# Idle bf16 identity products at the seams of the second cross attention in a two-block Perceiver kernel

## The chip, the cores and the metric

The kernel runs on one core of a Trainium2 chip. The metric is the device time of one execution in microseconds (us), from launch to completion. The core has a matrix engine (TensorE, PE in the profile, whose weight loads are a row of their own, PEld), VectorE (DVE), ScalarE (ACT), GpSimd (POOL) and SyncE (SP), which here issues most DMAs. The engines run their own instruction streams and meet on semaphores. The profile gives the clock that was granted to TensorE as a share of full speed: 1.00 is 2.4 GHz, 0.50 is 1.2 GHz.

## The reference

The input is x (16 x 64 tokens, width 256) and a context (16 x 1024 tokens, width 256). Two blocks are applied, with a residual sum and a layer normalisation around each step:

```python
x = x + L0_xattn(ln(x), ctx, ctx, mask, ...)   # 16 heads of 16, masked keys
x = x + L0_attn(ln(x), ...)                    # linear attention, 16 heads of 64
x = x + L0_ffn(ln(x), ...)                     # binarised weights, scale, bias, clip
x = x + L1_xattn(ln(x), ctx, ctx, ...)         # causal: 64 queries see keys 0..63
x = x + L1_attn(ln(x), ...)                    # gated delta rule with convolutions
x = x + L1_ffn(ln(x), ...)                     # 8 experts, the best one per token

def L1_xattn(query, key, value, Wq, bq, ...):
    q = (query @ Wq.T + bq)...; k = (key @ Wk.T + bk)...; v = (value @ Wv.T + bv)...
    scores = einsum('bhtd,bhsd->bhts', q, k) / sqrt(D) + causal
    return (einsum('bhts,bhsd->bhtd', softmax(scores), v)...) @ Wo.T + bo
```

The second cross attention is causal over 64 queries, so only the first 64 of the 1024 context tokens matter to it.

## The kernel before

The 1024 tokens are eight tiles of 128 (NT = 8), the width is two chunks of 128 (KC = 2). The program is four stages, one after the other, each a block in which every engine has one hand-written stream: `stage_abc` (the whole first block, and the keys `d_k` and values `d_v` of the second cross attention), `stage_d` (the second cross attention, and the gates of the gated delta rule), `stage_e` (the gated delta rule) and `stage_f` (the experts). At the end of a stage every engine drains, the engines meet, GpSimd clears the semaphores of the stage, and they meet again (lines 76, 80 and 81 of the profile). Nothing of a stage starts before that.

At the end of `stage_abc` the last products on TensorE are the output projection of the linear attention (L1168) and one product for the feed-forward step of tile NT - 2 (L1176). The feed-forward steps of the last two tiles are finished on VectorE inside `stage_d`.

`stage_d` runs over tiles t = 0 to 7 with a software pipeline of several tiles. The names that are needed:

- TensorE, before the loop: `turn_x(0)` (L1462, two transposes of the normalised tile), `queries(0)` (L1469, four products for the queries, two records each), then the transposes of `xc` (L1542) for the feed-forward step of the last tile, which wait for VectorE.
- TensorE, in iteration t: `scores(t)` (L1478, four bf16 products that lay the causal mask into banks 0 to 3, then L1486, 32 small products), for t = 0 the product of the feed-forward step (L1551, `cproj`), `turn_x(t + 1)`, `project(t - 2)` (L1519), `turn(t - 1, 0)` (L1498), `queries(t + 1)`, `turn(t - 1, 1)`, `weigh(t - 1)` (L1509, 64 small products).
- ScalarE copies the transposes out (`d_xt`, L1282), writes the scaled and biased queries block by block (`d_qbd`, L1288, four instructions), takes the exponentials (L1297) and copies the turned probabilities out (`d_pt`, L1303). The first copy of `d_xt` stands behind waits for two small GpSimd operations (L1256).
- VectorE, in iteration t: `shift(t, r)` for r = 0, 1 (L1378, the row maxima; L1380, the subtraction), for t = 0 the rest of the feed-forward step of the last tile (L1421, L1397 to L1401, and the moments), then `lengths(t, r)` (L1385, L1388), whose inverses GpSimd multiplies in (L1270).

`stage_e` begins on TensorE with L2144 (products of 8 columns) and L2158, the projections: 32 records of 128x512 before the first wait for another engine. ScalarE takes the first 1024 columns after eight of those records (`tap`, L1773), and VectorE convolves (L1954).

Every instruction of the stages stands in the order in which it is written; there is no planner. PSUM is eight banks of 512 float32 columns: in `stage_d` banks 0 to 3 hold scores, bank 4 the turned probabilities, bank 5 (`m_bank`) the transposed input and the queries, banks 6 and 7 the weighed values and others. `c.identb` is the 128x128 identity in bf16, loaded at the start of `stage_abc`.

Of the kernel before, what the change touches and what calls it, by code (L numbers as in the profile page):

```python
# [16 lines left out]
P = 128  # L17
B, S, D = 16, 64, 256
# [128 lines left out]
def stage_abc(nc, c):  # L147
# [6 lines left out]
    with stage_semaphores(nc) as ctx:  # L154
# [91 lines left out]
        bank = [ctx.enter_context(nc.psum_tensor(f"a_bank{i}", [P, 512], F32)) for i in range(8)]  # L246
        q_banks, k_banks, v_banks, t_banks = bank[0:2], bank[2:4], (bank[5], bank[6]), (bank[4], bank[7])
# [562 lines left out]
        def _(pe):  # L810
# [293 lines left out]
            for t in range(NT + 1):  # L1104
                if 0 < t < NT:
                    pe.wait_ge(U["xt"], t + 1)
                    pe.wait_ge(U["qt"], t)
                    for i in range(2):
                        dense(t, bwq, q_banks, i, U["qproj"])
                if 0 < t <= NT:  # L1110
                    pe.wait_ge(U["kh"], t)
                    if t == 1:
                        pe.wait_ge(T["xout"], NT)
                        pe.wait_ge(T["ot"], B)
                    else:
                        pe.wait_ge(U["ot"], t - 1)
                    turn_heads(kh, t_banks, U["ktp"])
                if t == NT:
                    fill(0)
                    fill(1)  # L1120
                if 0 < t < NT:
                    if t > 1:
                        pe.wait_ge(U["xout"], t - 1)
                    if t > 2:
                        pe.wait_ge(C["scaled"], t - 2)
                        pe.wait_ge(C["xt"], t - 2)
                    pe.wait_ge(U["xt"], t + 1)
                    for i in range(2):
                        dense(t, bwk, k_banks, i, U["kproj"])
                if 0 < t <= NT:  # L1130
                    attend_scores(t - 1)
                if t == NT:
                    fill(2)
                    fill(3)
                if 0 < t < NT:
                    pe.wait_ge(U["v"], t)
                    for i in range(2):
                        dense(t, bwv, v_banks, i, U["vproj"])
                if 0 < t <= NT:
                    attend_values(t - 1)  # L1140
                if t == NT:
                    fill(4)
                    fill(5)
                if t < NT:
                    pe.wait_ge(U["qh"], t + 1)
                    turn_heads(qh, q_banks, U["qtp"])
                if 0 < t < NT - 1:
                    pe.wait_ge(U["kh"], t + 1)
                    pe.wait_ge(NB["xn"], t + 2)
                    turn_tile(k_banks[1][:, 0:256], t + 1, U["xtp"])  # L1150
                if t > 1:
                    pe.wait_ge(NC_["xn"], t - 1)
                    if t == NT - 1:
                        pe.wait_ge(U["kh"], t + 1)
                    if t > NT - 1:
                        pe.wait_ge(C["scaled"], t - 2)
                    turn_tile(k_banks[1][:, 256:512], t - 2, C["xtp"])
                if t == NT:
                    fill(6)
                    fill(7)  # L1160
                if 0 < t <= NT:
                    pe.wait_ge(U["ot"], t)
                    if t < NT:
                        pe.wait_ge(U["kh"], t + 1)
                    else:
                        pe.wait_ge(U["xout"], t - 1)
                    for a in range(8):
                        m = pe.matmul(k_banks[0][:, 0:D], otb[:, a, :], bwo[:, a, :], start=(a == 0), stop=(a == 7))  # L1168
                    m.then_inc(U["oproj"], 1)
                if t > 1:  # L1170
                    pe.wait_ge(C["binary"], 1)
                    pe.wait_ge(C["xt"], t - 1)
                    if t < NT - 1:
                        pe.wait_ge(U["xt"], t + 2)
                    for kk in range(KC):
                        m = pe.matmul(k_banks[1][:, 0:D], xtc[:, t % 2, kk, :], wt[:, kk, :], start=(kk == 0), stop=(kk == KC - 1))  # L1176
                    m.then_inc(C["proj"], 1)


def stage_kit(nc, ctx, tag, banks=True):  # L1180
# [14 lines left out]
def stage_d(nc, c):  # L1195
# [4 lines left out]
    with stage_semaphores(nc) as ctx:  # L1200
        sb, sem, sems, _ = stage_kit(nc, ctx, "d", banks=False)
        ps = c.ps
        bank = [ps[:, i * 512:(i + 1) * 512] for i in range(8)]
# [255 lines left out]
        def _(pe):  # L1459
            def turn_x(t):  # L1460
                for k in range(KC):
                    m = pe.transpose(m_bank[:, k * P:(k + 1) * P], c.xn[:, t, k * P:(k + 1) * P], c.ident[:, :])  # L1462
                m.then_inc(z["xtp"], 1)

            def queries(t):
                pe.wait_ge(z["xt"], t + 1)
                for k in range(KC):
                    for kk in range(KC):
                        m = pe.matmul(m_bank[:, 256 + k * P:256 + (k + 1) * P], c.d_wq[:, kk, k * P:(k + 1) * P],  # L1469
                                      xt[:, t % 2, kk, :], start=(kk == 0), stop=(kk == KC - 1))  # L1470
                m.then_inc(z["qproj"], 1)
# [60 lines left out]
            def constants():  # L1532
                for k in range(KC):
                    pe.matmul(bank[4][:, 0:D], c.col("e_b2", k).to_broadcast([P, P]), c.e_w2[:, k, :], start=(k == 0), stop=(k == KC - 1))
                for k in range(KC):
                    pe.matmul(bank[4][:, D:D + E], c.f_small[2][:, :], c.f_small[0][:, k, :], start=(k == 0), stop=(k == KC - 1))

            turn_x(0)
            queries(0)
            pe.wait_ge(z["cxn"], 1)  # L1540
            for k in range(KC):
                m = pe.transpose(bank[6][:, k * P:(k + 1) * P], xc[:, k * P:(k + 1) * P], c.ident[:, :])  # L1542
# [2 lines left out]
            for t in range(NT + 3):  # L1545
                if t < NT:
                    scores(t)
                if t == 0:
                    pe.wait_ge(z["cxt"], 1)
                    for k in range(KC):  # L1550
                        m = pe.matmul(bank[7][:, 0:D], xtc[:, k, :], c.c_wt[:, k, :], start=(k == 0), stop=(k == KC - 1))  # L1551
                    m.then_inc(z["cproj"], 1)
                if t + 1 < NT:
                    if t > 2:
                        pe.wait_ge(z["ht"], t - 3)
                    if t + 1 > NT - 3:
                        pe.wait_ge(z["cxn"], t - NT + 5)
                    turn_x(t + 1)
                if 1 < t < NT + 2:
                    project(t - 2)  # L1560
                if 0 < t <= NT:
                    turn(t - 1, 0)
                if t + 1 < NT:
                    queries(t + 1)
                if t > 3:
                    if t == 4:
                        pe.wait_ge(z["weights"], 224)
                    pe.wait_ge(z["ht"], t - 3)
                    pe.wait_ge(z["ot"], min(t - 1, NT))
                    if t > NT:  # L1570
                        pe.wait_ge(z["gate"], t - 4)
                    gates(t - 4)
                if 0 < t <= NT:
                    turn(t - 1, 1)
                if t > 3:
                    pe.wait_ge(z["xout"], min(t - 1, NT))
                    decay_inputs(t - 4)
                if t > 2:
                    u = t - 3
                    pe.wait_ge(z["h"], u + 1)  # L1580
                    pe.wait_ge(z["qbd"], min(t + 2, NT))
                    if u:
                        pe.wait_ge(z["ht"], u)
                    for k in range(KC):
                        m = pe.transpose(m_bank[:, k * P:(k + 1) * P], h[:, u % 2, k * P:(k + 1) * P], c.ident[:, :])
                    m.then_inc(z["htp"], 1)
                if 0 < t <= NT:
                    if t > 1:
                        pe.wait_ge(z["ot"], t - 1)
                        pe.wait_ge(z["xout"], t - 1)  # L1590
                    else:
                        pe.wait_ge(z["csc"], 1)
                    if t > 3:
                        pe.wait_ge(z["gate"], t - 3)
                    weigh(t - 1)
                if t == NT + 1:
                    constants()


LEVELS = 6  # L1600
# [1138 lines left out]
```

## Time and profile before

| | |
|---|---|
| median of three runs | 699.14 us (697.95 to 700.17) |
| the profiled execution | 700.65 us |
| its span, first to last instruction | 698.9 us |
| around the span | 1.75 us |
| mean granted clock of TensorE | 0.935 |
| TensorE busy | 610.0 us (87%) |
| VectorE busy | 382.4 us (55%) |
| ScalarE busy | 333.5 us (48%) |
| GpSimd busy | 128.1 us (18%) |

All stretches in this document are given in us from the start of the span. `stage_abc` ends at about 343, `stage_d` at about 431, `stage_e` at about 580. The profiled execution took 1.5 us more than the median of the runs.

### The profile page before, as it was taken

The numbers are of one execution on the slowest core, as the hardware profiler recorded it, in microseconds if no ns is written. First come the engines' busy times: TensorE is split into PE (matmuls) and PEld (weight loads), VectorE is DVE, ScalarE is ACT, GpSimd is POOL, SyncE is SP. The second block draws the span as 40 slices with busy tenths as digits, with TensorE's granted clock in tenths as the row PEclk, the third lists the DMA queues.
The fourth block names the chain that finished last, engine by engine and source line by source line (L and its number), as shares of the span: only waits on it lengthen the run. The fifth ranks groups of instructions, "written<-read, shape, count | busy, mean of one in ns | idle before, by whom it ended". The sixth has DMA issues, their size and how long they took to land. (4 is left out here: it accounts for less than half of the span.)

```text
span 698.9 us, 20484 instructions
## 1 busy us (share of the span) xinstructions
PE 610.0 (87%) x8420; PEld 455.6 (65%) x8420; DVE 382.4 (55%) x911; ACT 333.5 (48%) x927; POOL 128.1 (18%) x192
## 2 busy tenths in 40 slices
PE   4779998999899999999777988988798986599995
PEld 2447666665466666666656765465798876498995
DVE  6426788875434545552267884879565783011211
ACT  1325655553444455444246764655365263144451
POOL 2002221001200000000223443424520204011111
PEclk9869999999999999999868999999789996799999
DMA  5950000000700000000230000000000007996110
GB/s 152 306 203 2 3 2 2 2 17 27 165 2 1 2 1 2 1 1 2 61 104 1 3 3 1 0 3 3 2 3 1 1 1 278 323 378 197 26 33 19
DMA packets 32717, 40.78 MB, mean 58 GB/s; under 512 B 8031, under 2 KB 28000, under 8 KB 32385
## 3 DMA queue, kind: packets, MB, share of 16 engines
q1 hardware_dynamic: 28672, 32.24, 14.2%
q0 software_dynamic: 1520, 4.38, 1.9%
q10 hardware_dynamic: 2448, 3.09, 1.6%
q8 instruction: 54, 0.88, 0.5%
q14 instruction: 23, 0.18, 0.1%
HBM read 35.33 MB, written 4.90 MB: 58 GB/s over the span
## 5 line engine op out<-in xcount | busy, mean ns | idle before, releaser
L390 ACT ACTIVATE a_pr<-a_bank,a_nms 128x160 f32<-128x160 f32 x128 | 49.2, 392 | 41.2 <-DVE a_nms L726 38.1
L2485 ACT ACTIVATE f_hb<-f_bank,cols 128x128 f32<-128x128 f32 x96 | 31.1, 368 | 59.7 <-PE f_bank L2596 38.1
L2596 PE MATMUL f_bank<-f_xts,f_w 128*128 x384 | 46.9, 282 | 9.0 <-ACT f_hb L2485 8.2
L2596 PEld LDWEIGHTS f_bank<-f_xts,f_w 128*128 128x128 f32 x384 | 46.4, 198 | 10.0 <-ACT f_hb L2485 8.4
L2606 PE MATMUL f_bank<-f_w,f_hb 128*128 128x256 f32 x192 | 46.4, 385 | 0.8 <-DVE f_yb L2565 0.8
L630 DVE TENSOR_REDUCE a_negmx<-a_bank 128x2 f32<-128x320 f32 x64 | 30.4, 475 | 22.8 <-PE a_bank L863 22.8
L2606 PEld LDWEIGHTS f_bank<-f_w,f_hb 128*128 128x128 f32 x192 | 35.3, 194 | 5.1 <-DVE f_yb L2565 1.2
L2557 DVE TENSOR_SCALAR f_xts<-f_bank 128x256 f32 x12 | 5.1, 424 | 60.8 <-PE f_bank L2588 60.8
L360 POOL TENSOR_TENSOR a_spr<-a_linv,a_hm 128x128 f32<-128x128 f32 x32 | 12.1, 400 | 123.9 <-DVE a_linv L679 111.1
L974 PE MATMUL a_bank<-b_wq,a_xtb 128*128 128x512 f32 x64 | 30.6, 624 | 2.9 <-ACT a_ct L483 2.9
L627 DVE COPY a_pt<-a_bank 128x512 f32<-128x512 f32 (+1 forms) x48 | 28.5, 593 | 7.9 <-PE a_bank L872 5.3
L410 ACT ACTIVATE a_lnv<-ln_mv,a_eps 128x1 f32<-128x1 f32 (+1 forms) x23 | 6.8, 295 | 52.6 <-DVE ln_mv L552 52.5
L1954 DVE SCALAR_TENSOR_TENSOR e_cv<-de_ps,cols,e_cv 128x1008 f32<-128x1008 f32 (+2 forms) x24 | 29.6, 1246 | 4.1 <-ACT e_cv L1773 3.5
L872 PE MATMUL a_bank<-ident,a_pr 128*128 128x128 f32 x128 | 21.8, 296 | 10.1 <-DVE a_pt L627 6.9
L2158 PE MATMUL de_ps<-e_ht,e_wqkv 128*128 128x512 f32 x64 | 30.4, 628 | 0.0
L789 DVE TENSOR_TENSOR x<-x,a_bank 128x256 f32<-128x256 f32 x8 | 3.4, 421 | 48.9 <-PE a_bank L1168 48.9
L1252 POOL MEMSET d_eps<- 128x1 f32 x3 | 0.2, 99 | 163.3 <-POOLq L81 163.3
L974 PE MATMUL a_bank<-b_wv,a_xtb 128*128 128x512 f32 x64 | 29.9, 607 | 0.0
L1168 PE MATMUL a_bank<-b_wo,a_pr 128*128 128x256 f32 x128 | 29.6, 384 | 0.1
L755 DVE TENSOR_REDUCE a_ss<-a_qbd 128x16 f32<-128x1024 f32 x16 | 19.4, 1215 | 18.3 <-ACT a_qbd L471 18.3
L974 PE MATMUL a_bank<-b_wk,a_xtb 128*128 128x512 f32 x64 | 29.0, 593 | 0.0
L471 ACT ACTIVATE a_qbd<-a_bank 128x512 f32<-128x512 f32 x32 | 17.3, 594 | 21.7 <-PE a_bank L974 21.7
(406 smaller groups left out, 1457.8 us busy)
## 6 DMA issues: line engine op xcount, KB each, us to landing
f_w<-in_f_w SPq DMA_DIRECT2D x16, 1024.0 KB, 10.8
a_ct<-in_ctxt SPq DMA_DIRECT2D x15, 160.0 KB, 4.4
slots<-a_zero POOLq DMA_DIRECT2D x1, 2210.0 KB, 12.1
f_xs<-slots ACTq DMA_DIRECT2D x14, 130.0 KB, 2.4
rows<-in_rows SPq DMA_DIRECT2D x1, 1096.0 KB, 8.1
x<-in_x SPq DMA_DIRECT2D x2, 512.0 KB, 5.4
b_wq<-in_b_wq SPq DMA_DIRECT2D x1, 1024.0 KB, 6.2
b_wk<-in_b_wk SPq DMA_DIRECT2D x1, 1024.0 KB, 8.3
```

The costliest lines, as they stand in the source:

```text
L390: i = act.activation(pr[:, p, j, k, :], s_bank[j][:, k * KW:(k + 1) * KW], ACT.Exp, bias=nms[:, p, j, k:k + 1], accum_out=rsum[:, p, 2 * j ...
L627: dve.tensor_copy(pt[:, a:a + n, :].rearrange("p a n -> p (a n)"), src[:, 0:n * P]).then_inc(done, 1)
L630: dve.tensor_reduce(negmx[:, p, j, :], s_bank[j][:, 0:KC * KW].rearrange("p (k n) -> p k n", n=KW), AXX, ALU.max, negate=True).then_inc(ne ...
L755: dve.reduce_sum(ss[:, g, :], sq[g].rearrange("p (h n) -> p h n", n=DA), AXX).then_inc(done, 1)
L872: m = pe.transpose(dst[:, (2 * jj + k) * P:(2 * jj + k + 1) * P], pr[:, p, 2 * g + jj, k, 0:KM], c.ident[:, :])
L974: m = pe.matmul(banks[i][:, :], xtb[:, t % 2, kk, :], wx[:, kk, i * 512:(i + 1) * 512], start=(kk == 0), stop=(kk == KC - 1))
L1168: m = pe.matmul(k_banks[0][:, 0:D], otb[:, a, :], bwo[:, a, :], start=(a == 0), stop=(a == 7))
L1954: a = dve.scalar_tensor_tensor(o_[:, :, back:S], src[:, :, 0:S - back], c.col("e_cw", 4 * m + 3 - back), o_[:, :, back:S], ALU.mult, ALU.add)
L2158: a = pe.matmul(ps[:, at + 512 * g:at + 512 * g + 512], wqkv[:, kk, m * P:(m + 1) * P], ht[:, kk, 512 * g:512 * g + 512], start=(kk == 0), ...
L2485: act.activation(hb[:, m, :], bank[m % 4][:, 0:P], ACT.Gelu, bias=c.col("f_b1", e * FC + m)).then_inc(z["act"], 1)
L2596: j = pe.matmul(bank[m % 4][:, 0:P], w1[:, e, kk, m * P:(m + 1) * P], xts[:, bass.ds(i % 2, 1), kk, :].rearrange("p b n -> p (b n)"), star ...
L2606: j = pe.matmul(bank[5][:, 0:D], hb[:, m, :], w2[:, e, m, :], start=(m == 0), stop=(m == FC - 1))
```

## The change

A function `warm` is added. It issues n products of the bf16 identity with itself (128x128 by 128x128) into columns of a PSUM bank that nobody reads before they are written again. Nothing waits for these products and they wait for nothing but their place in TensorE's stream. They are issued at six places: 12 at the end of TensorE's stream in `stage_abc`, 4 ahead of `turn_x(0)`, 10 between `turn_x(0)` and `queries(0)`, 8 between `queries(0)` and the wait for `xc`, 4 between `scores(0)` and the wait ahead of `cproj`, and 12 at the end of TensorE's stream in `stage_d`. That is 50 products. Nothing else changes.

```diff
                         m = pe.matmul(k_banks[1][:, 0:D], xtc[:, t % 2, kk, :], wt[:, kk, :], start=(kk == 0), stop=(kk == KC - 1))
                     m.then_inc(C["proj"], 1)
+            warm(pe, c, t_banks[0][:, 0:P], 12)
+
+
+def warm(pe, c, dst, n):
+
+    for _ in range(n):
+        pe.matmul(dst, c.identb[:, :], c.identb[:, :], start=True, stop=True)
...
+            warm(pe, c, bank[7][:, D:D + P], 4)
             turn_x(0)
+            warm(pe, c, bank[7][:, D:D + P], 10)
             queries(0)
+            warm(pe, c, bank[7][:, D:D + P], 8)
             pe.wait_ge(z["cxn"], 1)
...
                 if t == 0:
+                    warm(pe, c, bank[4][:, 0:P], 4)
                     pe.wait_ge(z["cxt"], 1)
...
                 if t == NT + 1:
                     constants()
+            warm(pe, c, bank[0][:, 0:P], 12)
```

## Rows read from the trace of the kernel before

**Rows 1.** The page, section 2: busy tenths and clock in 40 slices of the span.

```profile
PE   4779998999899999999777988988798986599995
...
PEclk9869999999999999999868999999789996799999
```

**Rows 2.** Stretches around the seams: length, busy us (records) of each engine, clock, DMA share, GB/s.

```profile
342.05:344.58 2.53, 0.00 (x0) 0.03 (x1) 0.74 (x2) 0.00 (x0) 0.04 (x2) 1.00 0.00 0
344.58:358.28 13.70, 11.52 (x66) 8.58 (x66) 10.09 (x22) 5.39 (x16) 5.38 (x13) 0.50 0.70 209
358.28:365.11 6.83, 3.72 (x50) 3.01 (x50) 5.10 (x11) 4.71 (x13) 3.09 (x4) 1.00 0.00 0
365.11:371.94 6.83, 6.53 (x108) 5.27 (x109) 2.35 (x4) 1.80 (x5) 0.88 (x1) 0.50 0.01 2
...
432.25:436.79 4.54, 4.54 (x10) 2.26 (x11) 1.06 (x3) 1.89 (x5) 2.47 (x12) 0.62 0.00 0
```

**Rows 3.** Waits of VectorE in 344.58 to 360: total us, times, longest.

```profile
DVE d_ngm L1378 <- PE de_ps L1486: 2.8, 2, 1.7
```

**Rows 4.** Timeline of the seam between `stage_abc` and `stage_d`: start, length, engine, line.

```profile
341.02 1.03 PE L1176 MATMUL a_bank<-c_wt,a_xtc 128*128 128x256 f32 x4
...
342.43 0.40 DVE L556 TENSOR_SCALAR xnorm<-x,ln_mv,ln_rs 128x256 f32<-128x256 f32 x1
...
344.58 0.63 PE L1462 MATMUL de_ps<-ident,xnorm 128*128 128x128 f32 x2 [2.53 <-PEq L81]
...
345.08 0.52 POOL L1256 TENSOR_TENSOR d_bq<-d_sc,cols 128x2 f32<-128x2 f32 x2
...
345.63 0.38 ACT L1282 ACTIVATE d_xt<-de_ps 128x256 f32<-128x256 f32 x1 [7.21 <-POOL d_bq L1256]
```

**Rows 5.** Timeline of the first two tiles of `stage_d`.

```profile
346.07 2.08 PE L1469 MATMUL de_ps<-d_xt,d_wq 128*128 128x128 f32 x8 [0.86 <-ACT d_xt L1282]
...
348.19 1.51 ACT L1288 ACTIVATE d_qbd<-de_ps,d_bq,d_sc 128x128 f32<-128x128 f32 x4 [1.75 <-PE de_ps L1469]
...
348.77 0.69 PE L1542 MATMUL de_ps<-ident,d_xc 128*128 128x128 f32 x2 [0.62 <-DVE d_xc L1407]
...
350.24 1.99 PE L1486 MATMUL de_ps<-d_k,d_qbd 32*128 32x64 f32 x32
...
352.28 0.69 DVE L1378 TENSOR_REDUCE d_ngm<-de_ps 128x8 f32<-128x512 f32 x1 [1.73 <-PE de_ps L1486]
...
357.24 1.50 ACT L1288 ACTIVATE d_qbd<-de_ps,d_bq,d_sc 128x128 f32<-128x128 f32 x4 [1.13 <-PE de_ps L1469]
...
358.67 0.20 DVE L1388 RECIPROCAL d_linv<-d_lsum 128x8 f32<-128x8 f32 x1
...
359.98 0.69 DVE L1378 TENSOR_REDUCE d_ngm<-de_ps 128x8 f32<-128x512 f32 x1 [1.11 <-PE de_ps L1486]
...
365.41 1.17 PE L1509 MATMUL de_ps<-d_pt,d_v 64*32 64x64 f32 x64 [2.09 <-ACT d_pt L1303]
...
367.48 1.99 PE L1486 MATMUL de_ps<-d_k,d_qbd 32*128 32x64 f32 x32
```

**Rows 6.** TensorE's timeline of a later tile at the full clock.

```profile
375.54 0.93 PE L1509 MATMUL de_ps<-d_pt,d_v 64*32 64x64 f32 x64 [1.78 <-ACT d_pt L1303]
376.41 0.61 PE L1478 MATMUL de_ps<-d_causal,identb 128*128 128x256 bf16 x4
376.95 1.12 PE L1486 MATMUL de_ps<-d_k,d_qbd 32*128 32x64 f32 x32
...
379.58 1.06 PE L1469 MATMUL de_ps<-d_xt,d_wq 128*128 128x128 f32 x8
```

**Rows 7.** Timeline at 408.67: four bf16 weight loads at the full clock.

```profile
408.67 0.33 PEld L1478 LDWEIGHTS de_ps<-d_causal,identb 128*128 128x128 bf16 x4
```

**Rows 8.** Timeline of the seam between `stage_d` and `stage_e`.

```profile
430.37 0.41 PE L1585 MATMUL de_ps<-ident,d_h 128*128 128x128 f32 x2
430.83 0.38 ACT L1348 ACTIVATE e_ht<-de_ps 128x256 f32<-128x256 f32 x1 [1.94 <-PE de_ps L1585]
...
432.25 0.58 PE L2144 MATMUL de_ps<-e_wab,e_ht 128*128 128x8 f32 x4 [1.46 <-PEq L81]
...
438.10 1.11 ACT L1773 ACTIVATE e_cv<-de_ps,cols 128x1024 f32<-128x1024 f32 x1 [2.05 <-PE de_ps L2158]
439.25 1.27 DVE L1954 SCALAR_TENSOR_TENSOR e_cv<-de_ps,cols,e_cv 128x1008 f32<-128x1008 f32 x1 [3.54 <-ACT e_cv L1773]
```

## The prediction

> **What bounds the kernel now.** I read the page first. Its row of busy tenths has TensorE at eight or nine tenths in most slices, and the clock row under it dips in a few places [rows 1]; two of the dips lie where the change puts products. The reader is to see that TensorE is both the busiest engine and the only one whose speed changes. Next I cut the time around the two seams into stretches by clock [rows 2]. From 342.05 to 344.58 TensorE has no product at all, at clock 1.00. The next 13.70 us are granted 0.50, although TensorE is busy in 11.52 of them. A second fall comes at 365.11 after a thin stretch (3.72 us busy in 6.83) and lasts 6.83 us. A third piece of half clock lies in the first microseconds of `stage_e` (mean 0.62 over 4.54 us). Then I asked who waits for whom in the first cold stretch: VectorE, which carries the first two tiles, waits 2.8 us in two pieces for the scores [rows 3]. Elsewhere in it VectorE is busy for 10.09 of 13.70 us. So a slow TensorE costs time here, but not all that it loses.
>
> **The first seam.** The last real product ends at 342.05, VectorE's last operation at 342.83, and the engines start again at 344.5 [rows 4]. The hole is the handover between the stages, not a wait for data. Twelve products now follow the last real one. No row shows a bf16 product of 128 columns with a load of its own, so I bound its pitch. The four bf16 masks of 256 columns take 0.61 us at the full clock with the drain of the last [rows 6], so their pitch is about 0.11 us, which is also 256 columns at 2.4 GHz; that is the upper end. Half the columns at half of that, 0.055, is the lower end. Four bf16 loads take 0.33 us, or about 0.08 each [rows 7], and as every product has its load I take 0.08. Twelve are 0.96 us, so TensorE is done at 343.0 instead of 342.05. VectorE had released the meeting only at 342.83, which hides all but 0.15 us (nothing at 0.055, 0.5 us at 0.11). The hole shrinks from 2.53 to about 1.7 us.
>
> The Trainium skill, TensorE: Matmul & The Clock Gate, section Back-to-back issue gap, gives 81 ns for each product of 128 columns in a stream of loads and products. By that page twelve would take 0.97 us, and the sum would be the same.
>
> **The start of `stage_d`.** Four products ahead of `turn_x(0)` take 0.32 us. ScalarE's first copy starts at 345.63, released by GpSimd's L1256 and not by the transposes [rows 4], so at the full clock they are free: the transposes end at about 345.3. The ten after `turn_x(0)` are 0.8 us, from 345.1 to 345.9, and the queries could not start before 346.07 [rows 5]. The eight after `queries(0)` are 0.64 us, ahead of a wait for VectorE that lasts until 348.77; the queries end at 347.1 at the full clock, so these too are covered. The four after `scores(0)` delay `cproj`, which VectorE needs only after its two shifts.
>
> **What the clock gives back, if it stays.** Compare the same work at either clock: the queries take 2.08 us cold and 1.06 warm, 32 score products 1.99 and 1.12, four masks about twice their 0.61 [rows 5, 6]. The chain for tile 0 is: VectorE's `xc` at 348.77, its two transposes (pitch 0.11 in place of 0.21), four masks (0.43 in place of 0.85), scores. TensorE reaches the scores at about 349.5 instead of 350.24; their operands from ScalarE are there at 348.8, since the queries end one microsecond sooner. Scores then end 0.87 us faster. The first shift starts at about 350.65 in place of 352.28: 1.6 us gained. From there VectorE has 6.6 us of its own work (352.28 to 358.87 [rows 5]), and at 359.98 it begins the next shift after 1.11 us of waiting for the scores of tile 1. These waited for ScalarE's `d_qbd` at 357.24, itself released by TensorE's queries. Warm, the queries of tile 1 end near 353.6 and ScalarE is held by the exponential behind VectorE's second shift (the two shifts take four times 0.69, until 353.4), so `d_qbd` runs from 354.0 to 355.5 and the scores are ready at 356.7, before VectorE is (357.3). The 1.11 us go too. Together 1.6 + 1.1 = 2.7 us, almost the 2.8 of [rows 3]. What is late next is VectorE itself, up to 362. Later tiles follow VectorE by way of `d_pt` and `weigh(0)` at 365.41, so the head start is carried on.
>
> **The second seam.** TensorE's stream ends at 430.78, ScalarE's at 431.21 [rows 8]. Twelve products are 0.96 us and end at about 431.75, 0.5 us behind ScalarE (0.2 at 0.055, 0.9 at 0.11). This delays the handover: a real cost, with nothing over it. Against it, in this execution the clock was down for the early projections: eight records of 512 columns should take about 3.6 us, and the first tap started at 438.10, 5.4 us after the projections began. If the clock stays, some 1.6 us of that come back at the tap and at VectorE's convolution at 439.25, and after that VectorE sets the pace of its chain. I take 1.5.
>
> **The sum.** Against the profiled execution: 700.65 - 2.7 - 1.5 + 0.15 + 0.5 = 697.1, and 0.2 less for the smaller transposes and masks of tile 1 that I left out, so 696.9. The median of the runs shown is 1.5 us below the profiled execution. I read that as an execution that had one cold piece more than most, and the fall at the second seam, after a hole of only 1.5 us, is the likeliest of them. Then the median has 2.7 to give and pays 0.65: 699.14 - 2.7 + 0.65 = 697.1, or 696.9 with the same 0.2. Both ways meet.
>
> **The rivals.**
>
> (B) The products do not hold the clock. Half a hole is still there (1.7 us of 2.53). For it: at the second seam the clock fell after only 1.47 us without products. Against it: that hole stands beside thin products of 8 columns, while here the TensorE before it is dense, and fourteen products follow within a microsecond of the restart. Then only the costs stay: 699.14 + 0.65, and about 0.4 us at the ten products, which at half clock are 1.1 to 1.6 us in a gap of 0.86: 700.0 to 700.4. The section HAM oscillation of the same page of the Trainium skill warns of longer standstills than the one here; by it the clock would not have fallen at 344.58 even without the products and they would buy nothing. The row shows that it fell.
>
> (C) The clock holds, but less arrives. Runs in which the fall came at another moment lose less, and the second fall stays or moves so that it covers more. If only the 1.6 us of the first shift arrive: 699.14 - 1.6 + 0.65 = 698.2.
>
> (D) More arrives: the second fall at 365.11 goes as well. From `weigh(0)` to the end of the scores of tile 2 the cold clock took 4.06 us (365.41 to 369.47 [rows 5]), the same work warm 2.53 (375.54 to 378.07 [rows 6]). With the rest up to 371.94 that is 1.5 to 2.5 us: 694.4 to 695.4. Against it: the hole there, 2.09 us before `weigh(0)`, has no product in it.
>
> (E) Slower. The handovers are paid in full: pitch 0.11 or more, clock down all the same, so that each product costs 0.2 us. Then the second seam alone is 12 x 0.2 = 2.4 less 0.4 of cover, the first 2.4 less 0.8, the ten products 2.0 less 0.9 of gap: 2.0 + 1.6 + 1.1 = 4.7, or 703.8. It decides from a pitch of about 0.14 us, where the three come to 1.3 + 0.9 + 0.5 = 2.7 us with no gain.
>
> **How the numbers follow.** A measurement of this kernel tells about 0.3% (2.1 us) from no change: faster is below 697.0, slower above 701.2. The forecast (A), 696.9 with its own range from 696.2 to 697.6, has 0.38; as it sits on the edge I count 0.31 as faster and 0.07 as the same. B has 0.17 and C 0.21, both the same. D has 0.17, faster. E has 0.07, slower. Faster 0.48, same 0.45, slower 0.07. The range takes in C and most of D and reaches to the near end of B: 694.9 to 699.7.
>
> **What would show it.** In the profile of the changed kernel: a clock of 1.00 from the first seam to the second tile; twelve bf16 records behind L1176 at a pitch near 0.08 us; the restart of `stage_d` at most 0.2 us later against L1176; the queries at 1.06 us, not 2.08; VectorE's wait for L1486 down from 2.8 us to under 0.3; a clock of 1.00 at L2158 and the handover there 0.5 us longer. Wrong would be a clock that still falls before `queries(0)`, or a first shift of tile 1 that does not move by more than 2 us against the restart.

## The result and the profile after

| | before | changed |
|---|---|---|
| median of the runs beside each other (8 and 8) | 699.65 us | 696.05 us |
| the profiled execution | 700.65 us | 695.91 us |
| its span | 698.9 us | 694.1 us |
| mean granted clock | 0.935 | 0.946 |

The ratio is 0.9951, with a 95% interval from 0.9927 to 0.9974: 3.4 us faster, between 1.8 and 5.1. Repeated later on 12 runs it was 0.9970 (0.9940 to 0.9999), or 2.1 us. One of those 12, at 704.27 us, was a slow run and is left out of the ratio.

First the stretches of the changed kernel round the seams, with the same columns as [rows 2].

```profile
341.36:343.89 2.53, 0.67 (x13) 0.52 (x10) 0.75 (x3) 0.00 (x0) 0.04 (x2) 1.00 0.00 0
343.89:352.94 9.05, 7.16 (x89) 6.08 (x90) 7.68 (x14) 4.05 (x13) 5.26 (x12) 1.00 0.87 281
352.94:356.35 3.41, 2.04 (x40) 1.47 (x37) 3.20 (x9) 1.92 (x5) 0.41 (x1) 1.00 0.44 99
356.35:359.76 3.41, 2.77 (x14) 2.72 (x14) 3.31 (x8) 2.35 (x6) 1.64 (x2) 0.50 0.00 0
359.76:370.00 10.24, 6.21 (x131) 5.09 (x130) 6.62 (x15) 6.95 (x19) 2.32 (x3) 1.00 0.01 2
370.00:376.83 6.83, 6.83 (x110) 5.54 (x111) 3.58 (x8) 2.94 (x11) 4.56 (x5) 0.50 0.01 2
414.38:417.79 3.41, 3.41 (x10) 2.12 (x9) 2.00 (x5) 1.59 (x5) 2.06 (x2) 0.50 0.00 0
430.47:436.00 5.53, 5.53 (x16) 2.80 (x17) 1.28 (x4) 3.01 (x6) 3.23 (x14) 1.00 0.00 0
```

The cold 13.70 us behind the first seam are gone, and so is the half clock at the start of `stage_e`. But there is a new fall at 356.35, 12.5 us behind the restart, in the second tile; the old second fall comes later; and there is one at 414.38, 70.5 us behind the restart, that the profile before does not have. That last one need not be due to the products: the fourth start of the run without any of them, r1 below, has one 71.4 us behind its restart. Products at the seams do nothing about the holes behind them.

The timeline of the first seam and the first tile. L1184 is the line of the idle products, and the lines behind it are shifted by the new code: L1469 is now `turn_x` (L1462 before), L1476 answers to L1469 of before, L1552 to L1542, L1493 to L1486, L1385 to L1378.

```profile
340.33 1.03 PE L1176 MATMUL a_bank<-c_wt,a_xtc 128*128 128x256 f32 x4
...
341.19 0.83 PE L1184 MATMUL a_bank<-identb 128*128 128x128 bf16 x12
...
343.89 0.38 PE L1184 MATMUL de_ps<-identb 128*128 128x128 bf16 x4 [1.86 <-PEq L81]
...
344.11 0.39 PE L1469 MATMUL de_ps<-ident,xnorm 128*128 128x128 f32 x2
...
344.33 0.72 PE L1184 MATMUL de_ps<-identb 128*128 128x128 bf16 x10
...
345.38 1.16 PE L1476 MATMUL de_ps<-d_xt,d_wq 128*128 128x128 f32 x8 [0.32 <-ACT d_xt L1289]
...
346.37 0.61 PE L1184 MATMUL de_ps<-identb 128*128 128x128 bf16 x8
...
348.08 0.44 PE L1552 MATMUL de_ps<-ident,d_xc 128*128 128x128 f32 x2 [1.09 <-DVE d_xc L1414]
...
348.88 1.12 PE L1493 MATMUL de_ps<-d_k,d_qbd 32*128 32x64 f32 x32
...
350.06 0.69 DVE L1385 TENSOR_REDUCE d_ngm<-de_ps 128x8 f32<-128x512 f32 x1 [0.62 <-PE de_ps L1493]
...
352.83 0.63 ACT L1304 ACTIVATE d_pr<-d_sh 128x512 f32<-128x512 f32 x1 [0.43 <-DVE d_sh L1387]
353.37 1.49 ACT L1295 ACTIVATE d_qbd<-de_ps,d_bq,d_sc 128x128 f32<-128x128 f32 x4
...
354.91 1.12 PE L1493 MATMUL de_ps<-d_k,d_qbd 32*128 32x64 f32 x32 [1.38 <-ACT d_qbd L1295]
```

From the start of L1176 to the restart of `stage_d` it is 343.89 - 340.33 = 3.56 us, as before (344.58 - 341.02 [rows 4]): the twelve products cost nothing. Twelve take 0.83 us with the drain of the last; one lasts 0.22, so the pitch is (0.83 - 0.22) / 11 = 0.055 us, the lower end of my bounds. The queries take 1.16 us in place of 2.08. The first row maximum starts 350.06 - 343.89 = 6.17 us behind the restart, before it was 7.70: 1.5 us gained. The last row shows where it is lost again: TensorE waits 1.38 us ahead of the scores of tile 1, for the queries that ScalarE writes (L1295) only behind an exponential that waits for VectorE's second shift (L1304). The clock fell at 356.35, at the end of that stretch.

VectorE's wait for the scores, the answer to [rows 3], in the same first two tiles:

```profile
DVE d_ngm L1385 <- PE de_ps L1493: 0.6, 1, 0.6
```

That is 0.6 us in place of 2.8, but not the under 0.3 that the prediction gave as a sign. What is left is the wait ahead of tile 0; the one ahead of tile 1 is gone.

The seam between `stage_d` and `stage_e`, beside [rows 8]. L2170 is the projection, L1785 the tap, L1966 the convolution.

```profile
428.35 0.42 PE L1596 MATMUL de_ps<-ident,d_h 128*128 128x128 f32 x2
428.61 0.83 PE L1184 MATMUL de_ps<-identb 128*128 128x128 bf16 x12
428.81 0.39 ACT L1355 ACTIVATE e_ht<-de_ps 128x256 f32<-128x256 f32 x1 [1.93 <-PE de_ps L1596]
...
430.47 0.58 PE L2156 MATMUL de_ps<-e_wab,e_ht 128*128 128x8 f32 x4 [1.03 <-PEq L81]
...
434.63 1.11 ACT L1785 ACTIVATE e_cv<-de_ps,cols 128x1024 f32<-128x1024 f32 x1 [0.35 <-PE de_ps L2170]
...
435.77 5.00 DVE L1966 SCALAR_TENSOR_TENSOR e_cv<-de_ps,cols,e_cv 128x1008 f32<-128x1008 f32 x4 [1.84 <-ACT e_cv L1785]
```

From ScalarE's last copy to the restart it is 1.66 us in place of 1.42: the products cost 0.24 us. From the restart to the first convolution it is 5.30 us in place of 7.00: 1.70 gained.

Set against the restart of `stage_d`, the two profiled executions compare like this (start of the row maximum of each tile, and of ScalarE's last copy `e_ht`):

| us behind the restart | tile 0 | tile 1 | tile 2 | tile 4 | last copy |
|---|---|---|---|---|---|
| before | 7.70 | 15.40 | 24.94 | 41.49 | 86.25 |
| changed | 6.17 | 12.68 | 20.65 | 38.88 | 84.92 |
| gain | 1.53 | 2.72 | 4.29 | 2.61 | 1.33 |

The two spans differ by 4.8 us, and only part of it lies where the products are. `stage_d` restarts 0.69 us earlier (343.89 against 344.58), although no product stands before L1176. From there 1.33 us are gained up to the last copy, 0.24 paid at the handover and 1.70 gained up to the first convolution. The remaining 1.3 us come behind it, where nothing was changed. In the eight traces of whole kernels of this study (this change, the kernel before and the variants below) `stage_d` restarts at 341.38 to 344.58, and from the first convolution to the end of the span it takes 258.3 to 261.2 us, on average 260.0 without the last twelve products and 260.0 with them.

### The profile page after: what moved, and what is told of

Same layout as the page of the kernel before. It is cut to its first block and busy times, and to the rows that moved or that the text cites. A ratio compares the mean times of both kernels' runs of the same rounds, so it can differ in the third digit from the quotient of the medians.

```text
span 694.1 us, 20584 instructions
## 1 busy us (share of the span) xinstructions
PE 606.1 (87%) x8470; PEld 455.2 (66%) x8470; DVE 383.2 (55%) x911; ACT 333.5 (48%) x927; POOL 128.1 (18%) x192
## 5 line engine op out<-in xcount | busy, mean ns | idle before, releaser
L974 PE MATMUL a_bank<-b_wq,a_xtb 128*128 128x512 f32 x64 | 28.9, 595 | 2.9 <-ACT a_ct L483 2.9
L1966 DVE SCALAR_TENSOR_TENSOR e_cv<-de_ps,cols,e_cv 128x1008 f32<-128x1008 f32 (+2 forms) x24 | 29.6, 1246 | 2.4 <-ACT e_cv L1785 1.8
L2170 PE MATMUL de_ps<-e_ht,e_wqkv 128*128 128x512 f32 x64 | 28.7, 598 | 0.0
L872 PEld LDWEIGHTS a_bank<-ident,a_pr 128*128 128x128 f32 x128 | 14.9, 151 | 19.4 <-ACT a_pr L390 11.7
```

Of the source, the lines that this page charges most:

```text
L872: m = pe.transpose(dst[:, (2 * jj + k) * P:(2 * jj + k + 1) * P], pr[:, p, 2 * g + jj, k, 0:KM], c.ident[:, :])
L974: m = pe.matmul(banks[i][:, :], xtb[:, t % 2, kk, :], wx[:, kk, i * 512:(i + 1) * 512], start=(kk == 0), stop=(kk == KC - 1))
L1966: a = dve.scalar_tensor_tensor(o_[:, :, back:S], src[:, :, 0:S - back], c.col("e_cw", 4 * m + 3 - back), o_[:, :, back:S], ALU.mult, ALU.add)
L2170: a = pe.matmul(ps[:, at + 512 * g:at + 512 * g + 512], wqkv[:, kk, m * P:(m + 1) * P], ht[:, kk, 512 * g:512 * g + 512], start=(kk == 0), ...
```

## The experiments

One profile is one draw: single executions of the kernel before took from 695.6 to 703.6 us, and the clock falls at other moments in each. So I measured in two ways, the time over many runs, and the distances above in every trace.

### One part alone

e1 leaves out the twelve products at the end of `stage_d`; e2 has these alone; e3 has only the twelve at the end of `stage_abc`; e4 only the 26 inside the first tile. Each is the changed kernel less some calls:

```diff
 e1, e4
-            warm(pe, c, bank[0][:, 0:P], 12)
 e2, e4
-            warm(pe, c, t_banks[0][:, 0:P], 12)
 e2, e3
-            warm(pe, c, bank[7][:, D:D + P], 4)
-            warm(pe, c, bank[7][:, D:D + P], 10)
-            warm(pe, c, bank[7][:, D:D + P], 8)
-                    warm(pe, c, bank[4][:, 0:P], 4)
 e3
-            warm(pe, c, bank[0][:, 0:P], 12)
```

> The change without the twelve products at the end of stage_d. Theory (two separate gains): from the restart of stage_d to the first row maximum of tile 1 it is as short as in the changed kernel, 12.7 us in place of 15.4 in the kernel before; the handover from stage_d to stage_e is 0.24 us shorter than with the products; where the clock falls at that seam the first convolution comes 7.0 us after the restart of stage_e, where it does not 5.3. Time about 2.5 us under the kernel before, 0.9965. Rival (the seam between stage_d and stage_e carries most of the gain): the time is within 1 us of the kernel before.

> Only the twelve products at the end of stage_d. Theory: the start of stage_d is as in the kernel before, 15.4 us from its restart to the first row maximum of tile 1 where the clock falls; the first convolution comes 5.3 us after the restart of stage_e at a clock of 1.00, 1.7 us sooner than before; the handover is 0.24 us longer. As the clock fell at this seam in the profiled execution before but need not fall in every one, the time gains 0.3 to 1.5 us: 0.998 to 0.9995. Rival: it carries most of the gain, 0.996.

> Only the twelve products at the end of stage_abc. Theory (what counts is how thin the whole stretch round the handover is): the twelve alone leave 1.9 us of handover and 0.9 and 0.6 us of waits behind it empty, so the clock still falls in most executions, perhaps a little later; 14 to 15.4 us from the restart to the first row maximum of tile 1; time 0.998 to 1.000. Rival (the handover itself was what let the clock fall, and bridging it is enough): 12.7 us and a clock of 1.00, with a time as in e1.

> Only the 26 products inside stage_d, none ahead of the handover. Theory: the handover of 2.5 us stays empty, so the clock falls at it or up to three microseconds later in many executions; then the dense start lets it come back sooner than the 13.7 us of the kernel before; 13 to 15 us from the restart to the first row maximum of tile 1; time 0.997 to 0.999. Rival (the thin start of stage_d lets the clock fall, not the handover): as e1, 12.7 us, 0.9965.

| | ratio to before (95%) | tile 1 | last copy | restart of `stage_e` to convolution |
|---|---|---|---|---|
| e1, all but the last twelve | 1.0006 (0.9988 to 1.0025) | 12.68 | 82.96 | 7.00 |
| e2, only the last twelve | 0.9970 (0.9946 to 0.9995) | 15.27 | 84.75 | 5.30 |
| e3, only the first twelve | 0.9997 (0.9970 to 1.0023) | 15.32 | 84.85 | 7.00 |
| e4, only the 26 inside | 0.9996 (0.9972 to 1.0020) | 12.67 | 84.85 | 7.00 |

In time the last twelve carry what can be measured, against my expectation, and the start products alone show nothing: for e1 and e4 I had expected about 0.9965 and 0.997 to 0.999. In the traces the split is clean all the same: 12.7 us to tile 1 with the 26, with or without the first twelve, 15.3 without. This is e3, the first twelve alone:

```profile
337.82 1.03 PE L1176 MATMUL a_bank<-c_wt,a_xtc 128*128 128x256 f32 x4
338.68 0.83 PE L1184 MATMUL a_bank<-identb 128*128 128x128 bf16 x12
341.38 0.43 DVE L1398 BATCH_NORM_STATS2 ln_st<-x 128x6 f32<-128x256 f32 x1 [1.75 <-PEq L81]
...
356.70 0.69 DVE L1385 TENSOR_REDUCE d_ngm<-de_ps 128x8 f32<-128x512 f32 x1 [1.03 <-PE de_ps L1493]
```

and its clock, in stretches:

```profile
343.50:353.70 10.20, 8.58 (x57) 6.70 (x56) 6.86 (x14) 3.60 (x10) 3.27 (x5) 0.50 0.89 269
```

The clock fell 2.1 us behind the restart, in the thin start of the stage. e4, the 26 alone, with the handover of 2.54 us left empty:

```profile
343.66 0.38 PE L1183 MATMUL de_ps<-identb 128*128 128x128 bf16 x4 [2.54 <-PEq L81]
...
343.66:356.10 12.44, 9.18 (x126) 7.56 (x126) 10.86 (x22) 5.97 (x17) 5.66 (x13) 1.00 0.73 231
356.10:369.70 13.60, 11.64 (x132) 9.92 (x132) 8.30 (x19) 6.75 (x17) 3.69 (x4) 0.50 0.01 1
```

The clock stayed over the handover and the first tile, as the rival had it and not my theory, and fell 12.4 us behind the restart for 13.6 us: the cold piece was moved by a tile, and of 2.7 us gained at tile 1, 1.0 us is left at tile 4 (40.50 us against 41.49). In e1 the same happens, but shorter:

```profile
344.55:358.30 13.75, 9.84 (x131) 8.15 (x132) 12.10 (x25) 6.73 (x20) 6.95 (x14) 1.00 0.72 210
358.30:368.60 10.30, 8.67 (x119) 7.02 (x118) 5.30 (x11) 5.06 (x12) 2.40 (x3) 0.50 0.01 2
```

### Four starts and four seams in one execution

To see each place at several moments of the clock I let `stage_d` and `stage_e` run four times, left out `stage_f`, and gave each `stage_e` a dense end like that of `stage_abc`:

```diff
-            stage_d(nc, c)
-            stage_e(nc, c)
-        stage_f(nc, c, out)
+            for rep in range(4):
+                stage_d(nc, c)
+                stage_e(nc, c)
+            with stage_semaphores(nc) as ctx:
...
+                    sp.dma_start(out[:, :].rearrange("(t p) d -> p t d", p=P), c.x).then_inc(done, 16)
 at the end of TensorE's stream in stage_e
+            pe.wait_ge(z["lgs"], 1)
+            for _ in range(40):
+                m = pe.matmul(bank[4][:, D:2 * D], c.ident[:, :], c.d_wo[:, 0, :], start=True, stop=True)
+            m.then_inc(z["filled"], 1)
+            warm(pe, c, bank[5][:, D:D + P], 12)
```

Two copies on VectorE wait for `filled`. The last line of the cut stands in r2 and r3 only, and as `stage_f` is missing the output is not the reference's. r1 has no call of `warm`, r2 has all of them, r3 all but the twelve at the end of `stage_d`, r4 these alone.

> No idle products. stage_d and stage_e run four times over in place of once, stage_f is left out and x is stored instead, and at the end of each stage_e TensorE has 80 dense float32 records and VectorE two copies behind them, as at the end of stage_abc; the output is not the reference's. It gives four starts of stage_d and four seams from stage_d to stage_e in one execution, each at another moment of the clock, and it is the base of the three kernels beside it. Expected about 1330 us; the clock falls at 3 or 4 of the 4 starts of stage_d in the first 3 us, and at 1 to 4 of the seams to stage_e. Where it falls at a start, 15.4 us from the restart to the first row maximum of tile 1, as in the kernel before; where it does not, 12.7.

> The same with all the products of the change at every start and seam, 200 in all. Theory (both seams give what the change's trace shows): 4 x 2.2 us at the starts and 4 x 0.6 at the seams, 11 us less than r1. Rival (what the start gains is lost again to a later fall, only the second seam gives): 3 to 5 us less than r1.

> The same with the products at the end of what precedes stage_d and in its first tile only. Theory: 7 to 10 us less than r1, with a clock of 1.00 at every start. Rival (lost again later, as the time of e1 says): within 2 us of r1, though the first tile is 2.7 us shorter at each start; the second fall then comes sooner, or lasts 10.2 us in place of 6.8.

> The same with the twelve products at the end of stage_d only. Theory: each handover 0.24 us longer, no fall at any of the four seams to stage_e, each fall so avoided 1.7 us; 1 to 6 us less than r1 according to how many of its seams fall. Rival (e2 was luck): within 1 us of r1.

The medians of six runs: r1 1372.11 us, r2 1365.97, r3 1366.81, r4 1365.21. The runs of one kernel spread over 6 to 12 us, so the three differences to r1 (6.1, 5.3 and 6.9 us, or 1.5, 1.3 and 1.7 for each of the four) tell that each part gives something over four starts or four seams, but not that the parts add up or that one gives more. r1 took 42 us more than I had forecast. None of the three differences fell in its forecast (11 us, 7 to 10, 1 to 6), nor in what the rivals gave (3 to 5, within 2, within 1). These are the first stretches of the four starts of r3, up to the fall and behind it:

```profile
345.40:359.20 13.80, 9.90 (x132) 8.21 (x133) 12.16 (x25) 6.74 (x20) 7.01 (x14) 1.00 0.70 209
359.20:369.40 10.20, 8.55 (x118) 6.83 (x118) 5.20 (x11) 5.02 (x12) 2.33 (x3) 0.50 0.01 2
601.40:615.10 13.70, 9.76 (x131) 8.10 (x132) 12.02 (x25) 6.74 (x20) 6.96 (x14) 1.00 0.65 209
615.10:625.40 10.30, 8.67 (x120) 6.98 (x119) 5.30 (x11) 4.98 (x12) 2.48 (x3) 0.51 0.01 2
854.50:867.70 13.20, 9.26 (x127) 7.60 (x127) 11.55 (x24) 6.56 (x20) 6.46 (x14) 1.00 0.68 217
867.70:871.20 3.50, 3.50 (x16) 3.14 (x16) 3.40 (x8) 2.57 (x7) 1.00 (x2) 0.52 0.00 0
1107.60:1120.30 12.70, 9.24 (x126) 7.58 (x126) 11.05 (x23) 6.10 (x18) 5.95 (x13) 1.00 0.75 225
1120.30:1123.80 3.50, 3.03 (x14) 3.03 (x15) 3.43 (x7) 2.53 (x7) 1.42 (x2) 0.52 0.00 0
```

Every one holds the clock for 12.8 to 13.9 us and then loses it. Over all traces that have exactly the change's 26 products inside `stage_d` (12 starts: the changed kernel twice, e1, e4, r2, r3) or none there (11: before, e2, e3, r1, r4), averages of the distances from the restart:

| us behind the restart | tile 1 | tile 4 | last copy |
|---|---|---|---|
| no products at the start (11) | 15.28 (14.47 to 15.40) | 40.91 | 85.57 |
| with them (12) | 12.68 (12.67 to 12.69) | 38.99 | 84.23 |
| gain | 2.6 | 1.9 | 1.3 |

The last two columns hide a split. The whole kernel has only the first start, the one behind `stage_abc`; starts two to four exist only in the kernels that repeat the stages.

| gain, us | tile 1 | tile 4 | last copy |
|---|---|---|---|
| first start (6 with, 5 without) | 2.7 | 1.3 | -0.1 (with 82.96 to 88.89, without 84.52 to 86.25) |
| starts two to four (6 and 6) | 2.6 | 2.5 | 2.8 (with 82.74 to 83.25, without 84.77 to 86.45) |

So r3 gains over r1 at starts that the kernel does not have, and at the one it has nothing is shown to be left at the end of `stage_d`. This agrees with the times of e1 and e4. Part of the loss at the first start is not the clock. In three of those six (the changed kernel's second trace, and r2 and r3) TensorE stands still twice for 0.5 to 1.1 us between tile 6 and tile 7, waiting for nothing that the profile shows, and tile 7 comes 9.86 to 10.14 us after tile 6 in place of 8.02. This is the changed kernel's second trace, at a granted clock of 1.00:

```profile
400.39 1.02 PE L1526 MATMUL de_ps<-d_wo,d_ot 128*128 128x256 f32 x4 [1.05 <-issue]
...
408.93 0.44 PE L1493 MATMUL de_ps<-d_k,d_qbd 32*128 32x64 f32 x5 [0.83 <-issue]
```

The first trace of the same kernel has no such pause. What they come from is open, and so is whether the products have a part in them: the 11 starts without products have none of half a microsecond or more, the first start of m3 below has them. Over the nine starts with products and without these pauses 2.1 us are left at the last copy.

Without products the clock fell at 0 to 3.1 us behind the restart in all 11; with the 26 it fell at 12.4 to 13.9 us in all 12. At the second seam, from the restart of `stage_e` to the first convolution: with the twelve products of 128 columns 5.30 us at all 16 seams, without 7.00 at 9 of 12 and 5.30 at 3. So the seam gives 0.75 x 1.70 - 0.24 = 1.0 us on average. With 1.3 us for the start, the average over all 12, the two together are 2.3 us or 0.9967 of 699 us, which lies in the intervals of both measurements of the change. With nothing for the start they are 1.0 us or 0.9986, inside the interval of the second measurement and of e2, but outside that of the first.

### Columns or instructions

```diff
-        pe.matmul(dst, c.identb[:, :], c.identb[:, :], start=True, stop=True)
+        pe.matmul(dst[:, 0:8], c.identb[:, :], c.identb[:, 0:8], start=True, stop=True)
```

> r2 with products of 8 columns in place of 128: the same 200 instructions and weight loads, a sixteenth of the columns. Theory (columns streamed, not instructions, keep the clock): as r1, 14.5 to 15.4 us to the first row maximum of tile 1 and 7.0 us to the first convolution at most seams. Rival (any instruction that keeps the sequencer going does it): 12.7 and 5.3 at all of them, as r2.

```profile
341.44 0.45 PE L1184 MATMUL a_bank<-identb 128*128 128x8 bf16 x12
```

There is one execution of this kernel, 1374.45 us, too few to speak of its time. The clock fell at all four starts, 2.2 to 3.2 us behind the restart, with 14.55 to 15.49 us to tile 1, as without products. It fell at two of the four seams to `stage_e`, where it falls at 9 of 12 without products: four seams are too few to say whether these products do anything there. The same number of products with the same weight loads held none of the four starts, where products of 128 columns held all 12. Narrower products also keep TensorE busy for less time (0.45 us against 0.83 for twelve), and the run does not separate the two.

### The holes behind the first tile filled too

```diff
 scores(t), behind the masks
+                if t == 1:
+                    warm(pe, c, bank[6][:, 0:P], 16)
 ahead of turn(t - 1, 0), and ahead of turn(t - 1, 1)
+                if t == 1:
+                    warm(pe, c, bank[6][:, 0:P], 8)
 ahead of weigh(t - 1)
+                    warm(pe, c, bank[6][:, 0:P], 24 if t < 3 else 8)
```

> The changed kernel and 128 more idle products in the second cross attention, in the holes that follow the first tile: for t = 1 16 ahead of the wait for the queries, 8 ahead of each of the two turns; 24 ahead of the weighing at t = 1 and 2, 8 at t = 3 to 8. Theory (in every start with the products of the change the clock fell 12.4 to 13.9 us behind the restart, in the thin second tile, and that took part of the gain back): no fall in the first 30 us of stage_d; first row maximum of tile 4 about 38.0 us behind the restart (38.9 in the changed kernel, 41.5 before); 1 to 1.5 us under the changed kernel. Rival (the products cost what they save, being queued ahead of the products that ScalarE releases): the same as the changed kernel or up to 1 us more.

> r2 (four starts and four seams, all products of the change) with the further products of m1. Theory: all four starts at 12.7 us to tile 1 and 37.5 to 38.3 to tile 4, no fall in the first 30 us; 3 to 6 us less than r2, 10 to 12 less than r1. Rival: within 2 us of r2.

> The changed kernel once more, beside m1 on the same chip. Theory (start 1.4 us, second seam 1.0 us): 0.9965 of the kernel before, between 0.995 and 0.998. Rival (the full 2.7 and 1.5 less 0.24): 0.9945.

m1 measured 0.9955 (0.9928 to 0.9982), the changed kernel beside it 0.9970 (0.9940 to 0.9999): lower, but the intervals overlap, so it is not shown to be better. m2 had a median of 1362.27 us, 3.7 under r2, likewise inside the spread. The clock did what the theory says. This is m1 in three stretches from the restart on:

```profile
343.80:374.00 30.20, 25.95 (x459) 22.55 (x460) 23.57 (x48) 17.93 (x50) 13.87 (x21) 1.00 0.33 97
374.00:404.00 30.00, 27.88 (x505) 21.73 (x503) 25.81 (x56) 23.35 (x69) 11.11 (x11) 1.00 0.01 2
404.00:430.00 26.00, 22.53 (x280) 16.05 (x276) 15.93 (x35) 12.88 (x44) 9.72 (x13) 1.00 0.01 2
```

The whole of `stage_d` ran at full clock. Tile 4 came at 36.58 us (38.88 in the changed kernel's profile, about 38.0 expected), the last copy at 82.92. But from tile 4 to tile 7 it took 25.38 us, where the changed kernel takes 24.06 at its best: 1.3 us more over three tiles, 0.44 for each, and 8 products at 0.055 us are 0.44. That fits products ahead of the weighing that stand on the path in those tiles. In m2 no start fell in the first 30 us either (it fell at 33.8 to 34.3), tile 4 came at 37.90 to 38.17 and the last copy at 84.24 to 86.53: no earlier than with the change (82.74 to 88.89). The rival held for the later tiles, the theory for the first three.

## Why the prediction held, step by step

The range and the sign held, and the forecast of 696.9 us was near: 696.05 us was measured, between the forecast's own range (from 696.2) and that of rival D (to 695.4), and the repeat at 0.9970 gives 697.0. Several steps were exact and two were not, and these two went opposite ways, so that the nearness of the number is in part luck.

**Right.** The costs on TensorE's stream: free at the first handover (0.15 forecast), free ahead of the queries and behind them, as ScalarE's first copy and VectorE's `xc` cover them. At the second seam 0.24 us was paid against 0.5; the pitch was 0.055 us, my lower bound, for which I had given 0.2. The chain of the first tiles: 1.6 us forecast at the first row maximum, 1.53 measured; 2.7 at tile 1, 2.72 measured in the profile, 2.6 on average. The second seam: 1.5 us forecast for an execution in which the clock falls, 1.70 measured.

**Wrong in part: "so the head start is carried on".** The clock falls later instead, 12.4 to 13.9 us behind the restart in 12 of 12 starts; before, it was already down there. Of 2.6 us at tile 1, 1.9 are left at tile 4 and 1.3 at the end of the stage, averaged over all starts. At the start that the kernel really has it is 1.3 at tile 4 and nothing at the end (-0.1, from six starts against five that spread over 5.9 and 1.7 us), in part through the pauses of TensorE shown above, which the prediction had not thought of. At the later starts of r2 and r3 the whole head start is carried on (2.8). A second fall that moves is what rival C said, and every start with the change's products has it. I had looked only at what the change's own stretches gain. The thin second tile stands in the trace of before, but at half clock, where the same work fills nearly twice the time (1.99 us against 1.12 for the scores) and leaves smaller holes.

**Wrong: how often the second seam falls.** I read the 1.5 us between the profiled execution and the median as one fall more than most, and gave the median nothing for the second seam. It fell at 9 of 12 seams without products, so it is worth 1.0 us to the median. The sum for the median was 2.7 - 0.65 + 0.2 = 2.25 us. With what the traces give it is 1.0 for the seam and between nothing and 1.3 for the start, so 1.0 to 2.3 us: one term was too large and another was missing, and they cancel at least in part.

**Rival B** (the products do not hold the clock) fell: the clock held for the first 12.4 us at 12 of 12 starts, and at 16 of 16 seams. What holds it at the start are the 26 products inside `stage_d`, which I had treated as covered extras. The twelve ahead of the handover did nothing visible: e4 held without them, e3 with them alone did not. These are one execution each, so that the empty handover is harmless is seen once. **Rival D** did not come by the change itself: its profile gained 4.29 us up to tile 2 because the second fall came later, and gave 1.7 of that back by tile 4. **Rival E**, slower, had no ground: its pitch of 0.14 us is two and a half times the measured one.

**Open.** The time of e1 is 1.0006 (0.9988 to 1.0025), where 1.3 us at the end of `stage_d` would be 0.998, just outside; nothing for the start would be inside. r3 against r1 does not speak against that, as its gain can come from the starts two to four. The spread from execution to execution, some 8 us, is larger than every part, and the times do not settle how the 3.4 us first measured divide. The distances in the traces settle it for tile 1 (2.6) and the second seam (1.0), not for the end of `stage_d` in the real kernel. What the later falls in `stage_e` and `stage_f` add or take was not tested.

## What to carry to other kernels

Idle products are cheap only in a hole that has another cause, and each one that stands ahead of released work costs its pitch. Filling a hole can move the next fall to the next thin stretch, as here in all 12 starts: look at the whole cold piece and at what lies behind it, at the density that the work will have at full clock, before counting its full price as gain. And where a clock that falls at another moment in each execution decides, one profile is one draw: repeat the stage inside one launch and count. But look at the first pass by itself: here it behaved otherwise than the passes behind it, and it is the only one that the kernel has.

## What the runs showed of the hardware

A bf16 product of 128 columns with its own load has a pitch of 0.055 us at the full clock, although the record of its load lasts 0.098 us: the loads overlap what stands beside them. I had expected 0.08 from the spacing of four loads [rows 7]. Twelve products of 8 columns take 0.45 us, twelve of 128 columns 0.83. With all the change's products at 8 columns the clock fell at 4 of 4 starts and 2 of 4 seams; with 128 columns it held for the first 12.4 us at 12 of 12 starts and at 16 of 16 seams. In one execution (e4) the clock stayed up over an empty handover of 2.54 us. In the changed kernel it fell behind a stretch in which TensorE had no wait over 1.4 us (352.94 to 356.35, busy in 2.04 of 3.41 us), and where that stretch and the next were filled (m1) it did not fall. TensorE can also stand still for about a microsecond at full clock with no wait that the profile shows (1.05 and 0.83 us in one trace of the changed kernel, none in the other).
